# Bias of the graph attention layer: added once per node tile to the features in the GRU sweep, in place of seven additions over batches of tiles at the end

## What is computed

```python
h = (x @ W).reshape(n, H, F)
e = leaky_relu(a_src[src] + a_dst[dst], 0.2)          # edges, and one self loop for each node
ex = exp(e - m[dst]); denom = segment_sum(ex, dst)
alpha = ex / (denom[dst] + 1e-16)
out = segment_sum(h[src] * alpha[..., None], dst)
y = out.reshape(n, H * F) + bias + x                  # the bias that is moved
y = relu(layernorm(y) * ln_gamma + ln_beta)
x = layernorm(x + y)
```

## Time and profile before

| | us |
|---|---|
| median of 3 runs | 7773.34 |
| lowest and highest | 7767.19, 7786.14 |
| span of the profiled execution | 8769.9 |
| DVE busy in it | 4844.9 (55%) |
| POOL busy in it | 5049.1 (58%) |
| PE busy in it | 6380.8 (73%) |

### The profile page before, as it was taken

The page is one execution under the profiler, slowest core; times in us unless marked ns, Lnnn a source line. Parts: engine busy times, 40 slices in busy tenths (PEclk is TensorE's granted clock), DMA queues, the critical chain, the costliest instruction groups (busy, mean ns, idle before and its releaser), DMA issues.

```text
span 8769.9 us, 105363 instructions
## 1 busy us (share of the span) xinstructions
PE 6380.8 (73%) x25864; PEld 4099.8 (47%) x25864; DVE 4844.9 (55%) x16703; ACT 2445.7 (28%) x7538; POOL 5049.1 (58%) x5303
## 2 busy tenths in 40 slices
PE   8977777789677876777776555556777776888881
PEld 4544555544455554444443333334444444666651
DVE  7974545554344443344443444434555557888888
ACT  4631111122011111111112222211222225666665
POOL 4656666600666665666665666656665545666650
PEclk9987878799789888888887767767898888999995
DMA  1013333344444444444456666663333335666662
GB/s 52 3 45 115 90 91 90 90 109 154 116 136 136 136 136 110 133 137 136 137 132 190 214 210 211 216 166 90 88 88 86 87 72 177 192 194 192 194 188 70
DMA packets 559179, 1141.73 MB, mean 130 GB/s; under 512 B 111895, under 2 KB 304380, under 8 KB 558462
## 3 DMA queue, kind: packets, MB, share of 16 engines
q0 software_dynamic: 249024, 659.51, 28.6%
q1 hardware_dynamic: 195886, 366.27, 12.0%
q10 hardware_dynamic: 113680, 109.21, 3.7%
HBM read 822.31 MB, written 312.26 MB: 129 GB/s over the span
## 4 chain that ended last, share of the span: by engine, by line
PE 40%; another core or an unknown queue 21%; DVE 16%; issue 14%; ACT 4%; DMA 1%; DVEq 1%; ACTq 1%; SPq 0%; POOL 0%; POOLq 0%
PE ps L1109 11%; PE ps L1331 6%; PE ps L1301 4%; PE ps L1519 4%; DVE AY L1783 3%; PE ps L1463 2%; PE ps L1506 2%; DVE edges L1650 2%; PE ps L1497 2%; PE ps L1492 2%; PE ps L1464 1%; PE ps L1098 1%; DVE AY L2069 1%; DVE edges L1649 1%
## 5 line engine op out<-in xcount | busy, mean ns | idle before, releaser
L1783 DVE TENSOR_TENSOR AY<-AY,ps 128x256 f32 (+1 forms) x4160 | 1744.1, 419 | 3173.0 <-remote 1681.1
L719 POOL DMA_INDIRECT g<-rel_d,edges x2496 | 2365.8, 948 | 1690.1 <-issue 672.4
L1109 PE MATMUL ps<-g,rows 128*128 128x256 f32 (+1 forms) x4160 | 1327.6, 440 | 278.7 <-DVE AY L1783 113.0
L1109 PE MATMUL ps<-g,oh 128*128 128x256 f32 (+1 forms) x4160 | 1373.7, 448 | 133.7 <-DVE oh L1766 35.7
L1109 PEld LDWEIGHTS ps<-g,rows 128*128 128x128 f32 x4160 | 835.4, 220 | 636.0 <-issue 381.6
L719 POOL DMA_INDIRECT g<-rows_d,edges x832 | 804.6, 967 | 544.4 <-issue 209.1
L719 POOL DMA_INDIRECT g<-in_x,edges x832 | 794.0, 954 | 442.0 <-issue 210.7
L1109 PEld LDWEIGHTS ps<-g,oh 128*128 128x128 f32 x4160 | 855.7, 224 | 396.3 <-issue 227.2
L1331 PE MATMUL ps<-AY,turned 128*128 128x512 f32 x1568 | 831.6, 658 | 174.6 <-ACT turned L746 83.9
L2056 DVE TENSOR_REDUCE AY<-ps 128x4 f32<-128x512 f32 x832 | 571.4, 687 | 177.4 <-PE ps L1497 114.0
L746 ACT ACTIVATE wt<-ps 128x512 f32<-128x512 f32 (+1 forms) x448 | 250.0, 559 | 1478.4 <-remote 625.1
(11 more groups left out here) (380 smaller groups left out, 9906.1 us busy)
## 6 DMA issues: line engine op xcount, KB each, us to landing
rel_d<-wt ACTq DMA_DIRECT2D x392, 256.0 KB
turned_d<-AY SPq DMA_DIRECT2D x104, 512.0 KB
wt<-turned_d SPq DMA_DIRECT2D x104, 512.0 KB
AY<-marks_d SPq DMA_DIRECT2D x104, 512.0 KB
rel_d<-g SPq DMA_DIRECT2D x49, 1024.0 KB
g<-rel_d,edges POOLq DMA_INDIRECT x2496
marks_d<-oh SPq DMA_DIRECT2D x104, 256.0 KB
marks_d<-rows SPq DMA_DIRECT2D x104, 256.0 KB
```

The source lines that it names most:

```text
L719: pool.indirect_dma_start(out=g[:, j, 0:width], out_offset=None, in_=table, in_offset=bass.IndirectOffsetOnAxis(ap=edges[:, word, c:c + 1] ...
L1109: ins = pe.matmul(sum_slot(order, j), one_hot_at(j % OHS), g[:, j, 0:width], start=True, stop=True)
L1783: dve.tensor_tensor(tile_at(A, t, width), tile_at(A, t, width), sum_slot(order, j), ALU.add)\
```

## The change

The instruction that takes the features out of PSUM was a multiplication by one; it becomes an addition of `bias3`. The addition of `bias3` over a batch of seven tiles in the tail is left out. The logits (L1979) still read the features from PSUM, without the bias.

```diff
                     if j == 9:
                         dve.wait_ge(s_prod[7], 1 + u + 1)
-                        dve.tensor_scalar(tile_at(A, bu), features, 1.0, None, ALU.mult)
+                        dve.tensor_tensor(tile_at(A, bu), features, bias3, ALU.add)
                         link.begin(dve.tensor_tensor(
                             att_tmp.rearrange("p (s d) -> p s d", s=2),
...
                     dve.wait_ge(s_share, i + 1)
                     link(dve.tensor_tensor(a, a, own[i], ALU.add))
                     link(dve.tensor_tensor(a, a, x, ALU.add))
-                    link(dve.tensor_tensor(a, a, over_batch(bias3), ALU.add))
                     first = spread_of(0, i, lambda j: A[:, TU * i + j, 0:D])
```

## The result

The changed kernel takes 7759.82 us (median of 20 runs, 7746.65 to 7768.88) against 7772.85 us of the kernel before (20 runs). The ratio is 0.9982, 95% interval [0.9977, 0.9988]: 0.18% faster, 14 us of the median before (the two medians lie 13.0 us apart). The forecast was 7759 us and 0.18%. A gain that I called hard to tell from none is told from none here, since 20 runs on each side give an interval of 0.06% to either side.

A forecast was written before the change was run, and what follows sets the result against it. No engine is full overall, but DVE bounds the tail. Profiled span 8769.9 - 14.4 + 0.3 + 0.0 = 8755.8 us; carried over, 7773.3 - 14.1 = 7759.2 us, 0.18% less, range 7741 to 7780.

The forecast's parts named there:

- The tail is DVE's own: Tail, last 175 us: DVE alone bounds it, so removing seven bias additions at 2.06 us each gains 14.4 us.
- 0.28 us given back to the table load: First batch of the tail: ACT's root is wanted 0.28 us before its table is in, so 0.28 us is lost.
- the line on what would show it: Expected signs in the changed profile, among them about 0.3 us of DVE idle time ahead of the first L2161.
- Middle roots late by 0.70 us: Middle tail batches: ACT's root comes 0.70 us late, but DVE's other work leaves 3.1 us of cover, costing nothing.
- L1978 keeps its length: GRU sweep: the edited line costs 419 against 418 ns, like L2004, 49 times, 0.05 us in all.
- 14.1 us carried over: Tail gain of 14.1 us taken unchanged from the profiled span, 12.8% above the median, to the measured time.
- the smaller gain of 12.5 us: Tail gain if the whole 12.8% excess of the profiled span were in the removed instructions too.
- A longer L1978 priced in full, 49 times: GRU sweep: any lengthening of L1978 counted at full length in each tile, with DVE's 4.08 us idle left out.
- the slower rival: GRU sweep: L1978 longer by 0.76 us or more, or a trip losing a microsecond; 35 us slower, 7808; chance 0.04.
- the one that hoped for a bonus: GRU sweep: unnamed waiting stretches become shorter by a slight shift, 15 us on top, 7744; chance 0.04.
- the stretch of 8.63 us: GRU sweep trip: ACT, and DVE for 4.08 us, waits for something the profile can't name.
- 0.16 for faster by over 0.3%: Chance given to over 0.3% faster: 0.13 by the spread of runs alone, 0.03 with the rivals.

The follow-up runs named there:

- execution of normal length: The kernel before, unchanged, profiled once more: ratio 1.0000 [0.9990, 1.0009], span 7775.6 us.

## Why the prediction was right, step by step

- *The tail is DVE's own, each addition on the path at 2.06 us, 14.4 us.* Right, and shown from two sides: 28 additions more cost 57.6 us, and leaving them out alone gives the whole gain.
- *0.28 us given back to the table load.* Right: the first L2161 waited 0.57 us against 0.28, and with an early table it was 0.28 again. Only the line on what would show it was put down wrongly: its "about 0.3 us of idle time of DVE" leaves out the 0.28 us that DVE waited for this root before.
- *Middle roots late by 0.70 us behind a cover of 3.1 us, at no cost.* Right: the root starts as L1062 ends, and 3.2 us of cover were left.
- *L1978 keeps its length, by the row of L2004.* Right: 417 ns. No fast form was lost.
- *14.1 us carried over from a span 12.8% too long, undiminished.* Right: the tail has the same length in both executions (175.4 and 175.6 us), so the smaller gain of 12.5 us was not needed.
- *A longer L1978 priced in full, 49 times, and the slower rival deciding from 0.76 us for each tile.* Wrong, though it was multiplied by zero in the sum. I read it from the earlier trace rows, where PE's transposes follow at once; that they wait for L1979 does not make the wait cost time, since POOL's issue of gathers sets the pace of the sweep. 2.25 us more in each tile cost some 9 us, where this price gives 49 x 2.25 = 110. The other half of that rival, and of the one that hoped for a bonus, rested on the stretch of 8.63 us in the earlier trace rows. In an execution of normal length the same wait of ACT is about 3 us and has a name (PE's transposes, L1457: 129.4 us in 40 times), so neither had ground.
- *0.16 for faster by over 0.3%, by spread.* The spread of three runs was what I had; the median over 20 left no such room.

## What to carry to other kernels

Look for the stage in which the edited instruction's engine is the only one at work. There a removed instruction is worth its pitch to the last tenth of a us, even where the engine is busy for 55% of the whole; then walk through each partner and ask whether it is ready earlier by as much. In a stage paced by another engine the same instruction is free up to a cover, and the end of the cover can be a step: look at who waits behind it, and at the granted clock behind that wait, over many trips and not in one. An idle engine is no free help either if its operands go through SBUF beside a busy DVE.

## What the runs showed of the hardware that I had not expected

- Seven-element DVE instructions of 0.17 us took 3.0 to 3.2 us beside POOL multiplications over 128x1792 (3.2 us each, one of 4.97 beside DVE's additions): the wait is about as long as the other engine's whole instruction.
- The granted clock fell to 0.50 behind a wait of PE of 4.6 us in all 34 trips, behind one of 3.2 us in 4 of 39, and behind the shorter one of 2.2 us (mean) in 21 of 39. Six products behind a fall took up to 2.77 us in place of 1.46.
- A fall of the clock cost some 1.6 us of a trip where PE's chain set the pace (23.4 us and more against 21.8), and next to nothing over two trips where the gathers did.
- Twenty transposes of the unit matrix, back to back, took 2.35 us; my estimate from the pairs in the trace was 4.1.
